# The last expert stage: three buffers for the up products, one bank for the down products, and the heads' rows spread by transfers within SBUF

## The reference, cut to what matters

```python
h = x @ Wm + bm
t = h.reshape(bs * L_ * H, HD)
w = jax.nn.softmax(t @ expert_emb, axis=-1)
topw, topi = jax.lax.top_k(w, 2)
hmid = jax.nn.gelu(jnp.einsum('td,edi->tei', t, W1) + b1, approximate=False)
eo = jnp.einsum('tei,eio->teo', hmid, W2) + b2
comb = (take_along_axis(eo, topi) * topw).sum(axis=1)
x = layernorm(x + comb.reshape(...) @ Wo + bo)
```

## Time and profile before

| | us |
|---|---|
| median of 3 runs (lowest, highest) | 3974.41 (3968.87, 3975.17) |
| the profiled execution | 3972.1 |
| its span | 3970.3 |
| from the stage's first instruction on SP (3123.75) to the first weights (3176.25) | 52.5 |
| from there to the end of the span | 794.05 |
| PE, ACT, DVE, POOL busy in these 794.05 | 716.60, 611.77, 339.60, 317.20 |
| TensorE's granted clock in the seven pieces from one chunk's weights to the next | 0.93 to 0.97 |

### The profile page before, as it was taken

The page is one execution under the profiler, slowest core; times in us unless marked ns, Lnnn a source line. Parts: engine busy times, 40 slices in busy tenths (PEclk is TensorE's granted clock), DMA queues, the critical chain, the costliest instruction groups (busy, mean ns, idle before and its releaser), DMA issues. The chain is left out here.

```text
span 3970.3 us, 46088 instructions
## 1 busy us (share of the span) xinstructions
PE 3419.3 (86%) x13440; PEld 1843.4 (46%) x13440; DVE 2705.4 (68%) x4289; ACT 1923.7 (48%) x2438; POOL 1926.2 (49%) x1197
## 2 busy tenths in 40 slices
PE   4666666699999999999958999999998599989998
PEld 1222222168888888888623333333333233333332
DVE  5998998745555555555539999999999544444443
ACT  3333333333333333333346566656663187777786
POOL 3555555423333333333237787768777144433343
PEclk7556565689999999999979999999999799999999
DMA  1000000000000000000002222222212122222222
GB/s 72 6 6 6 5 0 0 13 5 13 13 12 12 12 12 12 12 12 29 1 24 65 69 64 64 63 66 64 64 64 69 32 96 104 98 92 92 93 94 78
DMA packets 87494, 169.50 MB, mean 43 GB/s; under 512 B 8763, under 2 KB 10972, under 8 KB 86940
## 3 DMA queue, kind: packets, MB, share of 16 engines
q1 hardware_dynamic: 87324, 167.54, 12.3%
HBM read 160.96 MB, written 6.55 MB: 42 GB/s over the span
## 5 line engine op out<-in xcount | busy, mean ns | idle before, releaser
L1390 POOL TENSOR_TENSOR c_hc<-c_h,c_c_rep 128x1024 f32<-128x1024 f32 x256 | 603.8, 2365 | 223.8 <-DVE c_h L1443 201.3
L786 POOL TENSOR_TENSOR b_inner_low<-b_inner,b_inner_high 128x512 fp32r<-128x512 f32 x264 | 341.6, 1294 | 702.1 <-ACT b_inner_high L733 702.1
L1443 DVE TENSOR_TENSOR_SCAN c_h<-c_decay,c_carry,c_v_ps 128x512 f32<-128x512 f32 x512 | 629.6, 1264 | 0.0
L1809 ACT ACTIVATE d_hmid<-d_up,d_b 128x1024 f32<-128x1024 f32 x512 | 541.6, 1112 | 120.2 <-PE d_up L1713 119.2
L1163 PE MATMUL c_y_ps<-c_hc,ident 128*128 128x512 f32 x1024 | 531.3, 643 | 67.7 <-POOL c_hc L1390 64.6
L1848 POOL TENSOR_TENSOR d_acc<-d_acc,d_prod 128x512 f32<-128x512 f32 x240 | 317.2, 1322 | 526.3 <-DVE d_prod L1916 525.9
L855 DVE SCALAR_TENSOR_TENSOR b_acc<-b_ps,b_w_all,b_acc 128x256 f32<-128x256 f32 x1056 | 438.2, 478 | 180.8 <-PE b_ps L633 180.8
L1297 ACT ACTIVATE c_decay<-c_dt,c_a_cols 128x512 f32<-128x512 f32 x512 | 360.2, 719 | 401.5 <-DVE c_h L1443 394.5
L740 ACT ACTIVATE b_silu<-b_ps,b_pack 128x512 f32<-128x512 f32 x264 | 181.4, 687 | 757.1 <-PE b_ps L621 757.1
L345 POOL TENSOR_TENSOR a_hc<-a_h,a_c_rep 128x512 f32<-128x512 f32 x256 | 324.6, 1274 | 332.3 <-DVE a_h L381 317.9
L1916 DVE SCALAR_TENSOR_TENSOR d_prod<-d_eo,d_b,d_w_rep 128x512 f32<-128x512 f32 x240 | 180.2, 751 | 349.8 <-PE d_eo L1723 275.6
(11 more groups left out here) (235 smaller groups left out, 5941.9 us busy)
## 6 DMA issues: line engine op xcount, KB each, us to landing
c_c_rep<-c_c_scratch SPq DMA_DIRECT2D x256, 256.0 KB, 3.1
d_w_rep<-d_w_scratch SPq DMA_DIRECT2D x256, 256.0 KB
b_pack<-in_b_experts SPq DMA_DIRECT2D x33, 385.0 KB, 3.0
a_x_c<-in_a_x SPq DMA_DIRECT2D x8, 512.0 KB, 3.6
out<-xT SPq DMA_DIRECT2D x8, 512.0 KB, 5.6
xT<-in_xT SPq DMA_DIRECT2D x1, 3072.0 KB, 11.0
d_w_scratch<-d_w_t SPq DMA_DIRECT2D x8, 256.0 KB, 4.9
xT<-in_xT SPq DMA_DIRECT2D x1, 1024.0 KB, 5.0
```

What stands on the lines that cost most here:

```text
L786: nc.gpsimd.tensor_tensor(in_parts[1][:, c % IN, :], inner[:, c % 2, :], in_parts[0][:, c % IN, :].bitcast(F32), ALU.subtract).then_inc(in ...
L1390: nc.gpsimd.tensor_tensor(hc[:, q % HC], h[:, q % HR], c_rep[:, q % BC].unsqueeze(1).broadcast_to([P, PAIR, CH]), ALU.mult).then_inc(hc_re ...
L1443: nc.vector.tensor_tensor_scan(out=h[:, q % HR, m, :], data0=decay[:, i % DEC, :], data1=v_ps[m][:], initial=carry[:, i:i + 1], op0=ALU.mu ...
L1809: nc.scalar.activation(hmid[:, (2 * q + r) % HM], up_ps[r][:], ACT.Gelu, bias=b1[:, e:e + 1]).then_inc(gelu_ready, 1)
```

## The change

The PSUM banks are dealt out anew: three up buffers (six banks), one bank for the down products, and one bank `d_work` for everything that `d_work` and `d_norm` held. The buffer of up product i of a chunk is `slot[i]`, and `since[i]` names the product whose gelu must be done before it. down(q) now waits for weigh(q - 1).

The eight selection products and their eight copies are gone. Instead SP issues 32 transfers per chunk, each of 32 rows of 512 numbers (64 KB) from `parts` to `heads`, behind the weight load of step 8. The projections are made two chunks ahead instead of one, in steps 26 and 29. Since one bank is shared, new waits keep its users in a row: the logits wait for the centring, the variance waits for `route_max`, the transpose back waits for the deviation, the output projection waits for the projections' `low`. The transpose back moves from step 25 to 24, the logits from 13 to 11, the variance from 12 to 15. Ahead of chunk 0 stand the 32 transfers of chunk 0 and both projections of chunk 1.

```diff
-    HM, UP, EO, PR, WR = 4, 2, 2, 4, 8
-    Q_OUT, Q_RES, Q_MEAN, Q_CENTRE, Q_SQUARE, Q_VAR, Q_SCALE = 5, 6, 9, 9, 11, 12, 20
-    Q_HALF, Q_HIGH, Q_LOW, Q_HEAD, Q_COPY = 0, 0, 1, 4, 5
-    Q_LOGITS, Q_KEEP_LOGITS, Q_TURN, Q_MAX, Q_EXP, Q_PICK, Q_BACK, Q_KEEP_WEIGHTS = 13, 13, 15, 16, 17, 18, 25, 25
+    HM, UP, EO, PR, WR = 4, 3, 1, 4, 8
+    Q_SPREAD = 8
+    ROWS = P // DH
+    Q_OUT, Q_RES, Q_MEAN, Q_CENTRE, Q_SQUARE, Q_VAR, Q_SCALE = 5, 6, 9, 10, 11, 15, 20
+    Q_HALF, Q_HIGH, Q_LOW = 26, 27, 28
+    Q_LOGITS, Q_KEEP_LOGITS, Q_TURN, Q_MAX, Q_EXP, Q_PICK, Q_BACK, Q_KEEP_WEIGHTS = 11, 12, 13, 14, 17, 18, 24, 25
+    slot = [i % UP for i in range(2 * NU)]
+    slot[2 * NU - 1] = 1
+    since = [max(k for k in range(-2 * NU, i) if slot[k % (2 * NU)] == slot[i]) for i in range(2 * NU)]
...
-        work_ps = ctx.enter_context(nc.psum_tensor("d_work", [P, CH], F32))
-        norm_ps = ctx.enter_context(nc.psum_tensor("d_norm", [P, CH], F32))
+        work_ps = norm_ps = ctx.enter_context(nc.psum_tensor("d_work", [P, CH], F32))
...
+            def spread_heads(r, s, g):
+                sp.wait_ge(low_ready, r * GROUPS + g + 1)
+                if g == 0 and not (isinstance(r, int) and r < 2):
+                    sp.wait_ge(prod_ready, (r - 1) * NU + EO)
+                for j in range(HPG):
+                    for row in range(ROWS):
+                        sp.dma_start(heads[row * DH:(row + 1) * DH, s, g * HPG + j, :].bitcast(F32),
+                                     parts[j * DH:(j + 1) * DH, g, row // 2, :].bitcast(F32)).then_inc(head_loaded, 16)
             def chunk(c, s, first, last):
                 for q in range(NU):
                     spread(c, s, q)
+                    if q == Q_SPREAD and not last:
+                        spread_heads(c + 1, 1 - s, 0)
+                        spread_heads(c + 1, 1 - s, 1)
...
+            def logits(r, s, first):
+                pe.wait_ge(head_loaded, (r + 1) * HEADS * ROWS * 16)
+                if not first:
+                    pe.wait_ge(norm.zc_ready, (r - 1) * 2)
...
                 pe.wait_ge(prod_ready, c * NU + q + 1)
-                pe.wait_ge(gelu_ready, c * 2 * NU + 2 * q + 2 + UP)
+                pe.wait_ge(gelu_ready, c * 2 * NU + 2 * q + 2)
...
                         if q == Q_VAR:
+                            if not last:
+                                pe.wait_ge(route, (c + 1) * ROUTE + 2)
                             norm.variance(pe, c - 1)
                     if not last:
-                        if q in (Q_HALF, Q_HALF + 2):
-                            product(c + 1, 1 - s, (q - Q_HALF) // 2)
-                        if Q_HEAD <= q < Q_HEAD + HEADS:
-                            product(c + 1, 1 - s, HEAD0 + q - Q_HEAD)
                         if q == Q_LOGITS:
-                            product(c + 1, 1 - s, LOGITS)
+                            logits(c + 1, 1 - s, first)
                         if q == Q_TURN:
-                            product(c + 1, 1 - s, TURN)
+                            turn_logits(c + 1)
                         if q == Q_BACK:
-                            product(c + 1, 1 - s, BACK)
+                            turn_weights(c + 1)
+                        if q in (Q_HALF, Q_HALF + 3) and ahead(c):
+                            project(c + 2, (q - Q_HALF) // 3)
```

More of the change, by code:

```diff
@@ L1618, in layer1_experts, with ahead @@
         norm = Norm(nc, sb, sem, norm_ps[:], k, xT)
-        ROUTE, PICKS = 11, 7
+        ROUTE, PICKS = 12, 7
         NSPLIT = 6
+        def ahead(c):
+            return not (isinstance(c, int) and c + 2 >= NCH)
         block = ctx.enter_context(nc.Block())
@@ L1669, in _ @@
         def _(pe):
[L1670 to L1698, removed]
-                else:
-                    pe.wait_ge(route, (c + 1) * ROUTE)
-                    for b in range(BPC):
-                        last = nc.tensor.transpose(
-                            work_ps[:, b * P:(b + 1) * P],
-                            probs[:, b * HEADS:(b + 1) * HEADS, :].rearrange("p g e -> p (g e)"), k["ident"])
-                last.then_inc(work_ready, 1)
@@ new lines, in project @@
+            def project(r, g):
+                if g == 0:
+                    pe.wait_ge(wt_ready, r)
+                else:
+                    pe.wait_ge(low_ready, r * GROUPS + 1)
+                    pe.wait_ge(high_ready, r * GROUPS + 1)
+                for half in range(2):
+                    last = nc.tensor.matmul(work_ps[:], heads_w[:, half, g * P:(g + 1) * P],
+                                            xT[:, half, bass.ts(r, CH)], start=(half == 0), stop=(half == 1))
+                last.then_inc(projected, 1)
@@ new lines, in turn_logits, with turn_weights @@
+            def turn_logits(r):
+                pe.wait_ge(logit_kept, r + 1)
+                for b in range(BPC):
+                    last = nc.tensor.transpose(work_ps[:, b * P:(b + 1) * P], logit[:, b * P:(b + 1) * P],
+                                               k["ident"])
+                last.then_inc(turned, 1)
+            def turn_weights(r):
+                pe.wait_ge(route, (r + 1) * ROUTE)
+                if not (isinstance(r, int) and r < 2):
+                    pe.wait_ge(norm.log_ready, r - 1)
+                for b in range(BPC):
+                    last = nc.tensor.transpose(
+                        work_ps[:, b * P:(b + 1) * P],
+                        probs[:, b * HEADS:(b + 1) * HEADS, :].rearrange("p g e -> p (g e)"), k["ident"])
+                last.then_inc(turned, 1)
@@ L1707, in up @@
             def up(c, s, q, r):
                 e, g = q // GROUPS, q % GROUPS
-                if q == 0 and r == 0:
-                    pe.wait_ge(head_ready, (c + 1) * HEADS)
-                pe.wait_ge(gelu_ready, c * 2 * NU + 2 * q + r + 1)
+                i = 2 * q + r
+                if i == 0:
+                    pe.wait_ge(head_loaded, (c + 1) * HEADS * ROWS * 16)
+                if not (isinstance(c, int) and c == 0 and since[i] < 0):
+                    pe.wait_ge(gelu_ready, c * 2 * NU + since[i] + 1)
@@ L1820, in chunk @@
                     if not last:
-                        if q in (Q_HIGH, Q_HIGH + 2):
-                            high(c + 1, (q - Q_HIGH) // 2)
+                        if q in (Q_HIGH, Q_HIGH + 3) and ahead(c):
+                            high(c + 2, (q - Q_HIGH) // 3)
                         if q == Q_KEEP_LOGITS:
@@ L1835, in _ @@
             keep_weights(0)
+            for g in range(GROUPS):
+                high(1, g)
             over_chunks(act, NCH, chunk)
@@ L1925, in chunk @@
                 for q in range(NU + 1):
-                    if not last:
-                        if q in (Q_LOW, Q_LOW + 2):
-                            low(c + 1, (q - Q_LOW) // 2)
-                        if Q_COPY <= q < Q_COPY + HEADS:
-                            keep_head(c + 1, 1 - s, q - Q_COPY)
                     if q >= 1:
                         weigh(c, s, q - 1)
+                    if not last:
+                        if q in (Q_LOW, Q_LOW + 3) and ahead(c):
+                            low(c + 2, (q - Q_LOW) // 3)
                     if not first:
@@ L1987, in _ @@
                 route_pick(0, n)
+            low(1, 0)
+            low(1, 1)
             over_chunks(dve, NCH, chunk)
```

103 lines of the change are left out of this document (53 added, 50 removed).

## The result

| | before | after |
|---|---|---|
| median, us (lowest, highest) | 3974.79 (3968.87, 3975.45) | 4030.3 (4026.38, 4034.9) |
| the profiled execution, its span | 3972.1, 3970.3 | 4027.18, 4025.1 |
| ratio of the times, 95% interval | | 1.0143 [1.0126, 1.0161] |

The change makes the kernel 56 us slower; I had forecast 16 us faster, and 4030.3 lies above my range. The medians are those of four runs of each kernel on one chip.

The account below looks back on a forecast made before the run. Bound: ACT and PE waiting on each other each step, with four DMA engines' 88.1 us per chunk as floor. Terms -9 + 8.3 + 2.5 - 12 - 6 = -16 from the median 3974.41 gave 3958; range 3938 to 4012.

Parts of the forecast that it names:

- the issue term of the 32 transfers: After step 8's load: SP issues 32 transfers in 12 to 18 us, 15 taken, partly covered by outstanding loads.
- load 9: Later chunks, behind the weights copy: the load for step 9 lands at 41 us and is wanted at 43.
- Rival 1: The 32 transfers hold up weight loads while four engines idle: floor 99.9 to 106 per chunk, 4012 in all; chance 0.22.
- Rival 4: Three up buffers leave ACT at 2.25 per step, not 2.12, as down(q) waits for weigh(q - 1): 3986; chance 0.07.
- Rival 3: Single down bank costs more in steps 18 to 25, clock falls after the transpose in each chunk: 3968; chance 0.13.
- The floor of 88.1 in chunk 0: Weight loads on four DMA engines set a minimum of 88.1 us per chunk, on which chunks 0 and 1 lie.
- The walk of a middle chunk: Sum of ACT's steps, PE's blocks and waits in a middle chunk: 95.8 us against 97.83, a gain of 2.0.
- that at the transpose: ACT's gap at the transpose back, now behind down(23) and waiting on weigh(23)'s numbers: 4.6 us.
- the -2.4: Gain in us given to each of chunks 2 to 6, -12 together, the gap of 0.38 being a little wider there.
- the stage's start: Ahead of chunk 0, low part earlier and 32 issues instead of eight products and copies: -9 us (-5.8 to -11.5).
- the last stretch: From the last weights copy to the end, no transfers or picks: -7.1 and +1.1 for scale, so -6 us.
- The rule on small transfers: Skill page's 0.95 us per 64 KB: 32 in a row make 30 us per chunk, a time near 4120.

Follow-up runs that it names:

- 2 transfers: Changed kernel, but from chunk 2 on only 2 of a chunk's 32 head transfers are issued: 3985.3, ratio 1.0030.
- two and two buffers: Changed kernel with two up buffers and two down banks as before, all else as changed: 4030.02, ratio 1.0136.
- pairs and wide loads: Changed kernel with 16 transfers of two heads each (128 KB) and weights stored four times for loads with 16 outer rows: 3962.48, ratio 0.9968.
- thin transfers: Changed kernel, all 32 transfers, but from chunk 2 on each moves 64 of 512 columns (8 KB): 4023.33, ratio 1.0121.

## Why the prediction was wrong

**The step that failed** is the issue term of the 32 transfers: "SP issues one in 0.32 to 0.51 plus 0.05: 12 to 18 us, I take 15", some of it covered by the loads that are outstanding, and after it only 5.2 on the DMA engines. Two things were wrong in it. The price is 0.67, not 0.47, so 21.3 instead of 15; my bound of 18 came from loads of whole tiles, and these are transfers within SBUF of 32 rows, for which no row stood there. And I dated load 9 by the DMA engines ("lands at 41 and is wanted at 43"), not by SP, which can issue it only behind the 32 transfers. By SP it goes: eight loads and the ninth are issued until 23.5 behind the copy, then 21.3, then 6.4 until its weigh starts: 51.4, and it is wanted at 43.4 (3842.08). That is the 8 us. With my own 15 it would have been 44.9, so 1.5 late: the right order alone would have shown the cover too short, and the price made it 8. These 8 and the lower clock behind the standstill are about the difference of chunk 6 to the same chunk with 2 transfers (105.06 against 96.4).

**Rival 1** had the mechanism and the place (stalled four engines, weighs waiting for `w_rep` in every chunk, stretches above 99) and the wrong cause for it: the issues did not wait for the data of earlier ones, since they took 20.50 with an eighth of the bytes. It put 103 on a chunk, and chunks 1 to 6 took 102.5 to 109.2. I gave it 0.22, with its 4012 at the edge of my range, on the ground that the median issue took 0.51. Rival 4 (ACT does not reach 2.12) is refuted by ACT's ten gelus in 10.60. Rival 3 (the single bank costs more, and the clock falls behind the transpose) does not explain the 56 us, as the run with two and two buffers shows; but the half of it that is about the clock came true, and with pairs and wide loads, where no load is late, 3962.48 lies between my 3958 and its 3968.

**The floor of 88.1 in chunk 0** was read wrongly. Waits for `w_rep` 2.60 apart show that the transfers follow each other, not that they end last: with wide loads in the kernel before chunk 0 takes 74.71 instead of 74.93. In the changed kernel the loads are the bound, and chunk 0 costs 19.2 instead of 8.3; with loads in time it is 79.0 (pairs and wide loads), 4.1 above before, where my sum had 3.1 beside the floor. Chunk 1 costs 11.9 instead of 2.5, and 0.5 with loads in time.

**The walk of a middle chunk** held in its length and not in its gain. 95.8 was the sum, 96.4 is chunk 6 with 2 transfers and also with pairs and wide loads: 0.6 low. The gaps at PE's blocks are 1.72 (1.6), that at the transpose 5.0 to 5.6 (4.6), and behind it the clock does fall, which I had at 0.5 and which costs 1.6 (1.88 + 1.94 against 1.17 + 1.06). So one part of the change, the transpose one step earlier, costs about what the buffers bring: 38 against 35. I had counted its 4.6 and found a gain of 2.0 in chunk 6 and of 12 in chunks 2 to 6; measured with no load late are 1.4 in chunk 6, and in chunks 2 to 6 together 4.2 with 2 transfers and 1.2 with pairs and wide loads. So this term, too, was mis-sized: the -2.4 that I gave each of these chunks is 1.4 in chunk 6 and 0.7 or nothing in chunks 2 to 5.

At the stage's start 6.7 came instead of 9: the 32 issues take 20.57 where I had 15, and the logits follow 1.5 behind them where I had 3. In the last stretch 4.5 came instead of 6, and part of that may be luck: with the same work of the engines there it takes 121.4 in the changed kernel and 125.9 in those with few or thin transfers; in the last 22 us TensorE's granted clock is 0.91 in the former, 0.58 in the latter, 0.84 in the kernel before. What decides it is not shown. That pairs and wide loads come near my 3958 is luck, too, as far as the sum goes: the gain there lies at the stage's start (10.5 with 16 issues), and the seven stretches are 3.4 longer than before.

**The rule on small transfers.** A price of 0.95 us for 64 KB, a time of the DMA engines for loads issued by GpSimd (the Trainium skill, "DMA: Bandwidth & Descriptors", "Measured (HBM→SBUF, 128 partitions, SWDGE, issued from GpSimd)"), made 4120 by my estimate. It pointed the right way, by another path: what costs here is not that time but SP's, 0.67 per transfer, with 8 KB nearly as with 64 KB (20.50 against 21.29 for 32). That for so small transfers the count weighs more than the bytes, the runs bear out; the 0.95 they do not test.

## What to carry to other kernels

A DMA queue is an engine with a program of its own: date a load by the instruction that issues it, behind all that stands ahead of it in that queue, and only then by the DMA engines. Many small transfers put ahead of a stream of loads cost their number times the issue; merge them, and give the loads enough width to catch up: here each alone gave back 35 and 49 of the 56, and only both together kept every load in time. To issue the transfers from another engine's queue, or at another step, was not tried. Before a gain is put down to a buffer or lost to one, see that nothing else in the loop is late: the buffers here were worth 0 or 35 us, and the transpose's place 11, 27 or 38 us.

## What the runs showed of the hardware

- An issue of a transfer within SBUF from SP takes 0.52 at least and 0.59 in the median for 32 rows of 512 numbers, 0.60 for twice as many bytes, and 0.67 (8 KB: 0.64) by the span of 32 in a row. A weight load takes 0.507 at least; its median went from 513 to 653 ns in the changed kernel.

```profile
L1649 SPq DMA_DIRECT2D d_w_rep<-d_w_scratch x256: 507/653/5951, 3175.5 to 3987.3; - x128
L1657 SPq DMA_DIRECT2D d_heads<-d_parts x256: 519/591/2463, 3135.4 to 3843.0; - x128
```

- A load whose source has 4 outer rows moves 98 GB/s, a stream of loads with 16 outer rows and the same bytes came to 223. Storing the data four times and loading it wide changed nothing in the kernel before, 3973.39 against 3973.41; what the stores cost by themselves is not measured.
- PE's clock stayed at its upper level after waits of 1.12 and 1.65 and was at its lower one after waits of 3.31, and after the standstill of step 9. After a wait of 2.3 it was either: the first half of the last output projection ran at 0.53 in the kernel before (first row) and at 1.00 in the changed one (second).

```profile
3949.36 3.64 PE L1735 MATMUL d_norm<-d_acc,d_out_w 128*128 128x512 f32 x4 [2.26 <-POOL d_acc L1848]
4005.81 1.98 PE L1765 MATMUL d_work<-d_acc,d_out_w 128*128 128x512 f32 x4 [2.27 <-POOL d_acc L1884]
```

- Of the waits that DVE shows for a DMA, 40.4 us in the kernel before, 33 were taken away, and the time stayed.
